# Expert loads released by a GpSimd mark behind the row additions, in place of VectorE's count of down weights

## What is computed

```python
probs = softmax(xf @ router_weight)
topw, topi = top_k(probs, 8); topw = topw / topw.sum(-1)
# slot of each (token, expert) pair: its place in the expert's list, dropped from CAP on
xe = zeros(64, CAP, 512); xe[se, pos] = xf[tok]
h = silu(xe @ gate_proj[e]) * (xe @ up_proj[e])     # 512 -> 192
ye = h @ down_proj[e]                               # 192 -> 512
out[tok] += ye[se, pos] * weight                    # added to the layer's input
```

## Time and profile before

| | us |
|---|---|
| median of 3 runs | 1759.13 |
| the runs | 1756.70 to 1764.05 |
| the profiled execution | 1746.11 |
| its span, first to last instruction | 1744.3 |
| TensorE busy in the span | 1558.8 (89%) |
| VectorE busy | 1256.1 (72%) |
| ScalarE busy | 966.7 (55%) |
| GpSimd busy | 778.2 (45%) |
| mean granted TensorE clock | 0.95 |

### The profile page before, as it was taken

How to read it: one execution, slowest core, us unless ns; L and a number is a source line. 1 busy time by engine, 2 the same in 40 slices (tenths; PEclk the granted TensorE clock), 3 DMA queues, 4 the chain that set the end, 5 groups by cost and what they waited for, 6 DMA issues and landing times. The chain is left out here.

```text
span 1744.3 us, 25009 instructions
## 1 busy us (share of the span) xinstructions
PE 1558.8 (89%) x8016; PEld 1005.7 (58%) x8016; DVE 1256.1 (72%) x2994; ACT 966.7 (55%) x1938; POOL 778.2 (45%) x825
## 2 busy tenths in 40 slices
PE   5899999999999999999999996099988989888993
PEld 2444454455455455455445442089888878887883
DVE  2477778878878888888887874288767767776771
ACT  3455665665665676576566553056545545545551
POOL 4122325455456556456456557722323323323333
PEclk8889999999999999999999998589999999999997
DMA  9967653464464455335234220289999989998985
GB/s 332 293 187 252 218 161 115 135 214 126 140 203 126 136 169 148 113 111 150 75 93 117 65 65 23 97 266 269 257 247 241 260 240 234 249 248 236 261 210 69
DMA packets 145777, 311.89 MB, mean 179 GB/s; under 512 B 27162, under 2 KB 37274, under 8 KB 145648
## 3 DMA queue, kind: packets, MB, share of 16 engines
q1 hardware_dynamic: 106736, 238.89, 42.6%
q0 software_dynamic: 38912, 71.43, 19.5%
HBM read 141.25 MB, written 155.91 MB: 170 GB/s over the span
## 5 line engine op out<-in xcount | busy, mean ns | idle before, releaser
L1200 DVE TENSOR_REDUCE max_col<-bank 128x1 f32<-128x512 f32 x512 | 340.6, 682 | 148.0 <-PE bank L682 147.7
L964 ACT ACTIVATE p_t<-bank 128x512 f32<-128x512 f32 x512 | 294.3, 597 | 207.1 <-PE bank L691 203.1
L1520 POOL DMA_INDIRECT out_rows<-y_slots,row_ids x128 | 202.3, 1580 | 407.4 <-issue 364.8
L1479 POOL DMA_INDIRECT slot_rows<-row,slot_i x256 | 255.2, 997 | 77.0 <-issue 77.0
L691 PE MATMUL bank<-q_stack,k_stack 98*128 98x512 f32 x512 | 275.4, 540 | 10.3 <-DMA q_stack<-max_lo 6.1
L1467 POOL TENSOR_TENSOR p_sum<-p_t 128x512 f32<-128x512 f32 x128 | 167.6, 1315 | 194.5 <-ACT p_t L964 192.8
L800 PE MATMUL bank<-gate_up_hi,x_slots_t_hi 128*128 128x384 f32 x512 | 191.0, 373 | 51.3 <-DVE x_slots_t_lo L1327 51.3
L682 PE MATMUL bank<-k_stack,q_stack 96*128 96x512 f32 x512 | 211.8, 415 | 4.2 <-DVE max_col L1200 3.8
L691 PEld LDWEIGHTS bank<-q_stack,k_stack 98*128 98x128 f32 x512 | 96.8, 190 | 197.0 <-issue 172.0
L1327 DVE TENSOR_TENSOR x_slots_t_lo<-bank,x_slots_t_hi 128x512 fp32r<-128x512 f32 x128 | 88.0, 688 | 150.4 <-ACT x_slots_t_hi L1016 150.4
L1036 ACT ACTIVATE y_slots<-bank,x_slots 128x512 f32<-128x512 f32 x128 | 89.0, 696 | 192.0 <-DMA out_rows<-y_slots,row_ids 154.7
(11 more groups left out here) (185 smaller groups left out, 3059.2 us busy)
## 6 DMA issues: line engine op xcount, KB each, us to landing
gate_up<-in_gate_up SPq DMA_DIRECT2D x64, 768.0 KB, 7.5
slot_rows<-row SPq DMA_DIRECT2D x64, 577.0 KB, 8.1
x_slots<-slot_rows SPq DMA_DIRECT2D x64, 577.0 KB, 5.9
k_stack<-prob SPq DMA_DIRECT2D x192, 128.0 KB, 3.9
down<-in_down SPq DMA_DIRECT2D x32, 768.0 KB, 9.7
q_stack<-x_t SPq DMA_DIRECT2D x128, 128.0 KB, 2.4
x<-in_x SPq DMA_DIRECT2D x16, 512.0 KB, 3.3
ctx<-in_ctx SPq DMA_DIRECT2D x16, 512.0 KB, 5.1
```

Source lines behind the costliest of these rows:

```text
L964: e.activation(p_t[step % 2][:, h, :], psum[n % 2][:, :], ACT.Exp, scale=SCALE).then_inc(free[n % 2], 1)
L1200: e.tensor_reduce(max_col[quad % 2][:, h, c:c + 1], psum[2 + n % 2][:, :], X, ALU.max, negate=True).then_inc(free[2 + n % 2], 1)
L1479: e.indirect_dma_start(out=slots_dram, in_=rows[b % 2][:, k, :], in_offset=None, out_offset=bass.IndirectOffsetOnAxis(ap=slot_i[b % 2][:, ...
L1520: e.indirect_dma_start(out=out, out_offset=bass.IndirectOffsetOnAxis(ap=row_ids[e_ % NI][:, q, :].bitcast(U32), axis=0), in_=ye[e_ % NY][: ...
```

## The change

SyncE's turn e waits for a new semaphore, adds_issued, to reach e + 1. GpSimd counts it up: behind the second issue of each expert it runs a memset on a small tile of its own, issue_mark. Before that memset stands a wait for the mark of the expert before. The semaphore "added" is split by half, so each of ScalarE's copies into y_slots waits only for the addition that read the same half three experts ago; all who waited for both halves wait for both semaphores now.

```diff
-        added = [sem(f"added{i}") for i in range(2)]
+        adds_issued = sem("adds_issued")
+        added = [[sem(f"added{i}_{q}") for q in range(2)] for i in range(2)]
...
+        issue_mark = sb("issue_mark", [P, 1])
...
             for e_ in range(NEXP):
-                w.wait_ge(dn_lo_ok, min(e_ + 5, NEXP))
+                w.wait_ge(adds_issued, e_ + 1)
                 if e_ + NB < NEXP:
                     load_rows(e_ + NB)
                 if e_ + NB + 2 < NEXP:
                     load_weights(e_ + NB + 2)
             for i in range(2):
-                w.wait_ge(added[i], 32 * (NEXP // 2))
+                for q in range(2):
+                    w.wait_ge(added[i][q], 16 * (NEXP // 2))
...
                 if e_ >= NY:
-                    w.wait_ge(added[(e_ - NY) % 2], 32 * ((e_ - NY) // 2 + 1))
+                    w.wait_ge(added[(e_ - NY) % 2][s], 16 * ((e_ - NY) // 2 + 1))
...
                 if e_ >= NI:
-                    w.wait_ge(added[(e_ - NI) % 2], 32 * ((e_ - NI) // 2 + 1))
+                    w.wait_ge(added[(e_ - NI) % 2][0], 16 * ((e_ - NI) // 2 + 1))
+                    w.wait_ge(added[(e_ - NI) % 2][1], 16 * ((e_ - NI) // 2 + 1))
...
                     if e_:
-                        w.wait_ge(added[(e_ - 1) % 2], 32 * ((e_ - 1) // 2 + 1))
+                        w.wait_ge(added[(e_ - 1) % 2][0], 16 * ((e_ - 1) // 2 + 1))
+                        w.wait_ge(added[(e_ - 1) % 2][1], 16 * ((e_ - 1) // 2 + 1))
                 w.wait_ge(free[6 + q], full_a[6 + q] + e_ + 1)
                 e.indirect_dma_start(
                     out=out, out_offset=bass.IndirectOffsetOnAxis(ap=row_ids[e_ % NI][:, q, :].bitcast(U32), axis=0),
-                    in_=ye[e_ % NY][:, q, :], in_offset=None, compute_op=ALU.add).then_inc(added[e_ % 2], 16)
+                    in_=ye[e_ % NY][:, q, :], in_offset=None, compute_op=ALU.add).then_inc(added[e_ % 2][q], 16)
+                if q == 1:
+                    w.wait_ge(adds_issued, e_)
+                    e.memset(issue_mark[:, :], 0.0).then_inc(adds_issued, 1)
```

## The result

The changed kernel took 1754.43 us (median of 18 runs, 1749.97 to 1763.12), the kernel before 1759.95 (18 runs, 1753.34 to 1764.05). The ratio is 0.9974, with a 95% interval of 0.9962 to 0.9986: 4.6 us faster, where 16 were forecast. The gain is clear of the noise, but it lies within the 0.5% that was set as "no change".

The account below looks back on a forecast made before the run. The prediction took GpSimd's serial chain of row additions in the expert part as the bound. Its steps summed to 569.8 against 585.73 us, -16 us, taken from the median 1759.1 to 1743; range 1718 to 1790.

Parts of the forecast that it names:

- no change: Rival: the slowest DMA engine is full, so moving loads only changes which step is long; 1752 to 1763, chance 0.27.
- What bounds the kernel: Expert part: GpSimd's serial chain of row additions, 63 steps in 585.73 us, 9.30 us each, ends the kernel.
- The trigger (1): SyncE's load starts at the mark behind the second issue, 3.8 us into each step, against 5.08 and 5.60 before.
- The long step (2): Step with the light load: 10.2 us against 10.96 on average, from 9.57 plus 0.6 for the nearer light load.
- The short step (3): Step with the heavy load: 8.1 us, the middle between 7.75 and 8.57, giving a pair of 18.3 us.
- The sum's base (4): Whole chain: 9.0, 28 pairs at 18.3, 17.0 and 31.4 make 569.8 against 585.73 us: -16 us.
- The cost of the marks (5): GpSimd's 64 memsets of 0.10 us and one more wait per step are hidden in its idle time; uncovered, 25 us.
- The split (6): Split "added" semaphores let ScalarE copy a half one issue (1.85 us) earlier; worth 0 at the end.
- SyncE's other waits (7): Buffers of rows, gate_up and down pair are free when expert e's additions are issued; no new block on SyncE's queue.
- Sharing, the first rival: Loads right behind the second issue take turns with additions, landing them late; full price 1803, half 1774; chance 0.26.
- Starved TensorE: Rival: rows arrive later, TensorE waits 2.6 us a step; if that set the pace, 1818; chance 0.04.

Follow-up runs that it names:

- with one semaphore: The change with its split undone: the mark opens SyncE's turns, one "added" semaphore counts both halves; 1745.36 us beside 1758.41 before, ratio 0.9909.
- taking TensorE's waits away: Early mark and one semaphore, but SyncE's turn e opened one mark earlier, against the kernel before: 1834.42 us beside 1844.76, ratio 0.9940.
- with the light loads late: One semaphore, mark at once for heavy loads, 1.4 us later (1536 memset columns) for light ones, against the kernel before: 1789.49 us beside 1822.76, ratio 0.9822.
- the still later mark: One semaphore, light loads' mark delayed by a memset of 3072 columns, heavy ones' at once, against the kernel before: 1714.71 us beside 1759.13, ratio 0.9739.

## Why the prediction was wrong

The forecast was 16 us faster and the kernel was 4.6 us faster, an answer of "no change" by the bound of the text. The measured time, 1754, lies in the range of 1718 to 1790 and beside the rival "no change" (1757). One part of the mechanism was far too small, the overlap: the text saw that a load right behind the second issue runs into the tail of its own step's additions, but put this at 0.35 us for a heavy load (8.1 less 7.75) and 0.6 for a light one, and it costs 1.1 and 1.6 us. Point by point:

- **What bounds the kernel: right.** It is the chain of additions. Each first issue stands 0.84 us behind the landing of the additions before it (0.74 with one semaphore), and taking TensorE's waits away moved nothing.
- **The trigger (1): right.** Forecast 3.8 us into the step, measured 3.6 to 3.7. The memset is drawn 0.68 us long, not 0.10, but it begins while the second issue is still being drawn.
- **The long step (2): near, by luck.** Forecast 10.2, measured 9.96, from two errors that cancel. The base of 9.57 us was read from a step with the heavy load 3.70 us ahead of it. In the change the heavy load stands 5.6 us ahead (9.20 - 3.60), and with that and the light load at 5.1, as in the base, the step takes 8.33. And the light load close behind costs 1.6 us (9.91 against 8.33), where I took 0.6 between bounds of 0 and 2.31.
- **The short step (3): the step that failed.** Forecast 8.1, measured 9.20. I took the middle between 7.75 and 8.57 from a single early step. A heavy load right behind the second issue costs its own step 1.1 us (7.97 to 9.04), because its packets move between the last quarter of the additions. Over 28 pairs that is 31 us too little, less 7 for the long steps: 24. The chain of 63 steps was forecast at 569.8 us and took 591.5, 21.7 more.
- **The sum's base (4).** It went by the profiled run of before with 18.71 us per pair. The kernel before with an unused memset, equal to it in time (0.9997), had 18.92 in a run within 3 us of its median and a chain of 593.7 us (1154.48 to 1748.15), where the profile of before has 585.7. The 8 us between them go far to explain why the profiled runs make the change look slower and the timed runs make it faster. The gain of the first steps was right: expert 0 to 6 took 54.9 us (63.2 before), and the forecast gave 9.0 + 2.5 pairs of 18.3, 54.8. For the first seven steps the text says "about 6" us where its own sum gives 7.6; measured were 7.0 (71.54 to 64.52). These first steps are all of the change's gain. Against the kernel with the unused memset the change is 9.0 us shorter in the first six steps, 4.4 longer from there to expert 54 and 2.5 longer behind it.
- **The cost of the marks (5): right**, nothing, shown by the memset that nobody waits for.
- **The split (6): a second term put at nothing that is not nothing.** ScalarE's earlier copies were worth nothing at the end, as the text says. But GpSimd has two waits in the chain in place of one, and they cost 0.10 us a step, 6 us, which are part of the 21.7. The text did not see either that the split alone costs 39 us.
- **SyncE's other waits (7): nearly right.** From 1205 to 1745 its loads of gate_up waited 4.9 us in all, in six waits, for VectorE to be done with a buffer.
- **Sharing, the first rival**, is what took the gain. It came in at two fifths of its full price: the pair at 19.15, between the forecast's 18.3 and the full 20.45. It holds for the last quarter of the additions only. The Trainium skill ("DMA: Bandwidth & Descriptors", "Queues, rings and completion order") says that an engine takes turns between queues that have work, a packet at a time. The trace agrees in part: at the end of the additions 34 and 47 packets of the load move between theirs in 2 us. It does not agree in the long steps of before, where the additions move no packet for 4 us behind the load's 281. I had set the rule aside because of these long steps, and they say nothing about a load that comes behind the additions.
- **Starved TensorE: fallen.** TensorE does wait for rows (64.0 us), and without these waits the time is the same. A sign that I had named for it did appear, GpSimd "waiting for y_slots" (141.7 us in 24 pieces), as in the row at 1426.10. With one semaphore and the same loads this reads "issue" (350.0 us) and 24.8 us. But for expert 0 (20.4 us) it is a wait for several semaphores that the view puts down to a wrong releaser: the copies that these first issues need had ended 17 us and more before, while the 0.84 us to the landing holds there too.
- **No change** named the right time for a reason that is not the one: it held that the DMA engines' slowest member is full. Its sign did appear, a share of 0.92 as before. But the engines were not full: with the light loads late and the same transfers their mean share is 0.97 and the kernel is 1.8% faster than before, and with the still later mark 2.6%.

## What to carry over

In this kernel a serial chain of small slow transfers shares the DMA engines with large loads. What paid was to place each load so that it starts when the chain's current transfer is nearly done and ends before the next one needs the engines. A load that is too large for the gap should start early, since to delay it cost more (1.80 us) than it saved (1.07), and a load that nearly fits should start late; one trigger for both cannot do that. A wait that is added to a serial chain is paid at every link, 63 times here, however idle its engine is. And a bound that is taken from one or two steps of a trace should be kept whole: the middle of it was where this forecast lost its gain.

## What the runs showed of the hardware

A second semaphore wait ahead of an indirect DMA of GpSimd costs 0.10 us from the landing to the issue: 0.84 us with two semaphores in four traces, 0.74 with one in six, and nearly the same at every step of a trace.

A wide memset on GpSimd holds up some of VectorE's instructions. In the kernel with 3072 columns VectorE's cast to down_hi, 428 ns in the mean in the kernel before, took 3.91 us while the memset ran:

```profile
1422.65 3.24 POOL L1527 MEMSET issue_mark<- 128x3072 f32 x1
```

```profile
1422.26 3.91 DVE L1366 CAST down_hi<-down 128x512 fp32r<-128x512 f32 x1
```

Its mean over 54 instances rose to 1197 ns. Copies and casts that met such a memset took 2 to 3.9 us; the tensor-tensor instructions hidden (0.29 us) and hidden_t_lo (0.41 us) took no longer than without it. The kernel was 2.6% faster than before all the same, but it makes a memset a poor clock. The Trainium skill ("Trainium Architecture — The Big Picture", section "What this means for kernel authors") states that VectorE and GpSimd share a port under an exclusive lock; for the casts these rows agree, and for the two kinds that kept their time they do not.

Chips differ in a part of the kernel: with equal code up to the expert part, the first issue of additions came at 1151.83 us on one chip, at 1214.02 on a second and at 1240.50 on a third, while the four last steps took 7.70 to 7.99 us on all of them. Only ratios to a kernel on the same chip could be used.
